# Plain attention stage: V runs one or two steps later, sixteen probability buffers, the copy of the sums two exponentials later

## What is computed

```python
qh = qh / sqrt(HD)                               # 16 heads of 16, S = 512
scores = einsum('bqhd,bhkd->bhqk', qh, kh)       # per head 512 x 512, no causal mask
attn = softmax(where(mask, scores, -inf), axis=-1)
ctx = einsum('bhqk,bkhd->bqhd', attn, vh)
x = x + (ctx @ Wo.T + bo)
```

## Time and profile before

| what | value |
|---|---|
| three runs | 2143.11, 2147.13, 2151.1 us, median 2147.13 |
| profiled execution | 2140.8 us, its span 2139.1 us |
| busy in the span | PE 81%, DVE 62%, ACT 52%, POOL 20% |
| first exponential of stage a0 | 142.97 us |
| last DVE operation of stage a0 | 493.56 us |

### The profile page before, as it was taken

The page is one execution under the profiler, slowest core; times in us unless marked ns, Lnnn a source line. Parts: engine busy times, 40 slices in busy tenths (PEclk is TensorE's granted clock), DMA queues, the critical chain, the costliest instruction groups (busy, mean ns, idle before and its releaser), DMA issues. The chain is left out here.

```text
span 2139.1 us, 40029 instructions
## 1 busy us (share of the span) xinstructions
PE 1741.3 (81%) x13902; PEld 1065.8 (50%) x13903; DVE 1331.3 (62%) x2355; ACT 1113.6 (52%) x1985; POOL 425.6 (20%) x415
## 2 busy tenths in 40 slices
PE   7659999997967999969710299999999349999987
PEld 4412222225733444437610288888888125655554
DVE  5559999984655777827844244444444367777753
ACT  6328888884525777754313233333333235565551
POOL 5200000003302233337638400000000522222000
PEclk9869999999988999987655699999999679999999
DMA  6511111102421332211268211111111421111000
GB/s 193 158 44 31 38 39 39 37 7 85 132 93 49 84 88 86 66 29 61 72 222 281 99 46 48 45 49 46 48 45 45 129 79 52 51 50 49 20 11 20
DMA packets 116771, 153.21 MB, mean 72 GB/s; under 512 B 18184, under 2 KB 96416, under 8 KB 116640
## 3 DMA queue, kind: packets, MB, share of 16 engines
q1 hardware_dynamic: 110496, 134.70, 20.2%
q0 software_dynamic: 6144, 16.79, 2.3%
HBM read 92.40 MB, written 58.53 MB: 71 GB/s over the span
## 5 line engine op out<-in xcount | busy, mean ns | idle before, releaser
L1005 ACT ACTIVATE a_prob<-a_psE 128x512 f32<-128x512 f32 (+2 forms) x896 | 453.9, 575 | 135.1 <-PE a_psE L908 132.9
L1025 DVE TENSOR_REDUCE a_nm<-a_psS 128x2 f32<-128x1024 f32 (+1 forms) x384 | 442.5, 1176 | 43.7 <-PE a_psS L886 28.7
L908 PE MATMUL a_psE<-Q,K 51*128 51x512 f16 (+3 forms) x1024 | 281.4, 347 | 32.4 <-DMA Q<-a_nrow 20.5
L886 PE MATMUL a_psS<-K,Q 49*128 49x512 f16 (+4 forms) x1024 | 267.9, 359 | 32.6 <-DVE a_nm L1025 14.8
L1643 ACT ACTIVATE ex_hf<-ex_psH,ex_b 128x256 f32<-128x256 f32 x312 | 130.7, 470 | 234.2 <-PE ex_psH L1675 234.2
L1675 PE MATMUL ex_psH<-ex_xT,ex_w1h 128*128 128x256 f16 x1872 | 231.9, 274 | 4.8 <-ACT ex_xT L1634 2.1
L924 PE MATMUL a_psO<-a_prob,vall 128*32 128x512 f32 (+3 forms) x2048 | 228.0, 529 | 3.8 <-ACT a_prob L1005 0.7
L1689 PE MATMUL ex_psY<-ex_w2h,ex_hl 128*128 x1872 | 229.5, 273 | 1.0 <-DVEq L1600 0.4
L1610 DVE CAST ex_hl<-ex_hf 128x512 f16<-128x512 f32 x156 | 66.6, 427 | 258.1 <-ACT ex_hf L1643 258.1
L908 PEld LDWEIGHTS a_psE<-Q,K 51*128 51x128 f16 x1024 | 74.9, 94 | 262.7 <-ACT a_prob L1005 166.1
L1675 PEld LDWEIGHTS ex_psH<-ex_xT,ex_w1h 128*128 x1872 | 180.5, 98 | 31.2 <-issue 9.7
(11 more groups left out here) (282 smaller groups left out, 2958.9 us busy)
## 6 DMA issues: line engine op xcount, KB each, us to landing
s_qk<-t_pk SPq DMA_DIRECT2D x32, 512.0 KB, 3.1
ex_stage<-in_w SPq DMA_DIRECT2D x16, 1024.0 KB, 5.9
s_xs<-a_zero SPq DMA_DIRECT2D x32, 312.0 KB
ex_xt<-s_xs SPq DMA_DIRECT2D x39, 256.0 KB, 2.6
s_ys<-ex_yo SPq DMA_DIRECT2D x39, 256.0 KB, 2.2
t_xin<-in_x SPq DMA_DIRECT2D x16, 512.0 KB, 4.7
K<-s_qk SPq DMA_DIRECT2D x64, 128.0 KB
Q<-s_qk SPq DMA_DIRECT2D x64, 128.0 KB
```

What stands on the lines that cost most here:

```text
L886: last = pe.matmul(psS[:, bank, col:col + n], Q6[s][at:at + SROWS, pr, t * P:(t + 1) * P], K6[s][at:at + SROWS, pr, 0:n], start=True, stop ...
L908: last = pe.matmul(psE[unit % NE][:, col:col + w], K6[s][at:at + EROWS, pr, t * P:(t + 1) * P], Q6[s][at:at + EROWS, pr, S - w:S], start=T ...
L1005: act.activation(prob[:, unit % NP_BUF, 0:w], psE[unit % NE][:, 0:w], ACT.Exp, scale=ESC).then_inc(p_ready, 1)
L1025: dve.tensor_reduce(nm[G % NM_BUF][:, t, :, i], psS[:, at:at + 2, 0:n], axis=AX.X, op=ALU.max, negate=True).then_inc(s_free, 1)
```

## The change

It has four parts, all for the plain stage: the number of `prob` buffers, the table of the V runs, the step that the code behind the loop looks up in this table (the last V run), and the exponential behind which the copy of the sums stands.

```diff
-    NP_BUF, NE, NM_BUF = 24 if causal else 12, 3, 4
+    NP_BUF, NE, NM_BUF = 24 if causal else 16, 3, 4
...
     WEIGH_AT = ({4: ((-1, 2), (-1, 3)), 10: ((0, 0),), 14: ((0, 1),)} if causal else
-                {2: ((-1, 3),), 6: ((0, 0),), 10: ((0, 1),), 14: ((0, 2),)})
+                {4: ((-1, 3),), 8: ((0, 0),), 12: ((0, 1),), 15: ((0, 2),)})
...
-            for g, t in WEIGH_AT[4 if causal else 2]:
+            for g, t in WEIGH_AT[4]:
                 weigh(G_ALL - 1, t)
...
-                    if k == (5 if causal else 3) and G > 0:
+                    if k == 5 and G > 0:
                         evacuate(G - 1)
```

## The result

The changed kernel took 2154.51 us (median of 10 runs, 2148.68 to 2157.8); the kernel before, run beside it, 2144.17 us (10 runs, 2139.03 to 2153.09). The ratio is 1.0042, 95% interval 1.0024 to 1.0061: slower, by 5 to 13 us. The forecast was 2162.8 us, 15.7 us slower.

What follows compares the result with a forecast made beforehand. No engine was full; a chain through PE, ACT and DVE set the 10.82 us group period. It would grow to 11.38: 28 x 0.56 = 15.7 us on the 2147.13 median gives 2162.8, own range 2156 to 2170, 8-in-10 range 2147 to 2172.

Steps and rivals of the forecast that it cites:

- Step (2): Turn directly behind V run 0: ends at 3.10, division starts late at 3.13, top 4 at 3.95, top 5 at 5.09.
- The ring: Chain through PE, ACT and DVE from exponential 5 to the next group's: period 11.38 instead of 10.82, 0.56 us more.
- Step (1): Copy of the sums and V run 0 move by two alike; distance from exponential to V run stays 1.12.
- Step (3): V run 2 now behind S(14), which waits for top 5: PE stands 0.52, S(15) at 7.69, top 7 at 8.14.
- Step (4): Next group's S(2) waits for top 7, then E(4), V run of step 4, exponential 5 at 11.38, closing the period.
- Steps (5) and (6): Sixteen buffers instead of twelve, and the row copy with its DMA behind the later turn: each costed at nothing.
- Step (7): First and last groups, 4 of 32, leaving 28 steady periods: ends taken as nothing, 2 us either way in the range.
- The sum: Whole forecast effect over the steady groups of stage a0: 28 x 0.56 = 15.7 us slower.
- no change: Rival: V run 2 gets past the held S(14), period 10.85, 28 x 0.03 = 1 us, time 2148; chance 0.12.
- the faster ring: Rival: DVE not late, only PE and ACT's ring counts, period 10.46, -10.1 us, time 2137.0; chance 0.06.
- The clock: Rival: PE waits more and its clock falls; half clock in a third of groups adds 26 us, 2189; chance 0.05.

Runs made afterwards that it cites:

- run 0: Not a follow-up run: V run 0 is the kernel's V run with t = 0, at step 6 in the kernel before and step 8 in the changed one.
- e5: Kernel before with only V run 1 moved, from step 10 to 12; ratio to before 0.9968 (0.9953 to 0.9984), period 10.59 us.
- e2: Kernel before with only V run 2 moved, from step 14 to 15; ratio to before 1.0049 (1.0035 to 1.0062), period 11.23 us.
- e1: Changed kernel with V run 2 back at step 14 instead of 15; ratio to before 0.9993 (0.9981 to 1.0006), period 10.78 us.
- e3: Changed kernel with twelve probability buffers instead of sixteen; ratio to before 1.0027 (1.0014 to 1.0041), period 11.06 us.
- e6: Kernel before with sixteen probability buffers instead of twelve; ratio to before 0.9998 (0.9980 to 1.0017), period 10.83 us.
- e7: Kernel before, unedited, profiled a second time; stage a0 took 375.5 us and stage a1 306.8 us.

## Why the prediction was right and wrong

The step that failed is (2): its leg from the division to top 4 (0.82 taken, 0.64 measured) and its start of the turn (1.00 behind V run 0 taken, 0.88 measured). The ring itself is the one that was forecast.

- Step (1), the distance from exponential 5 to V run 0: 316.99 - 315.86 = 1.13, forecast 1.12. Right.
- Step (2), the turn behind the V run makes the division late: the mechanism was right, two terms were mis-sized, and they are the whole miss. First, the turn was to start 1.00 behind the V run's start, the distance of a shifted score. It starts 317.87 - 316.99 = 0.88 behind it: -0.12. Second, division to top 4 was taken as 315.26 - 314.44 = 0.82 and measured 319.52 - 318.88 = 0.64: -0.18. In the kernel before that leg held a wait that I read as work: S(8) and S(9) had been held and were released together at 314.58, and top 4 came 0.45 after E(10)'s slot at 314.81, not after the recorded start of S(9). A row that the earlier trace rows leave out shows the wait, the second operation of the division in the kernel before:

```profile
314.72 0.42 DVE L1049 TENSOR_TENSOR oall<-a_psS,a_rc 128x256 f32<-128x256 f32 x1
```

It ended at 314.72 + 0.42 = 315.14, and DVE stood idle until top 4 at 315.26, 0.54 behind the start of this row. In the new order both scores are done when the division ends, and top 4 starts at once: 319.52 - 319.18 = 0.34. e5 and e2 have the held pair and legs of 0.81 and 0.79, e1 and the changed kernel have it not and show 0.64. 11.38 - 0.12 - 0.18 = 11.08; measured 11.06.
- Step (3), S(14) waits for top 5, V run 2 and S(15) behind it: right, shown by e1 and e2. PE's wait there is 0.28 (E(15) goes at 310.57, S(14) at 310.85), forecast 0.52; it shrank by most of what step (2) had too much. DVE's idle times, 0.60 and 0.35, were forecast as 0.7 and 0.4 to 0.5.
- Step (4), top 7 to S(2), E(4), the V run, exponential 5: 1.29, 0.22, 0.31, 1.42, forecast 1.28, 0.23, 0.31, 1.42. Right.
- Steps (5) and (6), buffers, row copy and its DMA: nothing, as forecast (e3, e6; E(0) is not late in the changed kernel).
- Step (7), the ends: of the last three steps between copies of the sums the first fell to 10.67 from 10.83, the next was 10.14 instead of 9.87, the last 7.79 instead of 8.62. The stage grew by 7.6 against e6 and e7, 0.9 more than the 28 periods. The forecast of nothing with 2 us either way holds.
- The sum: 28 x 0.24 = 6.7 us in place of 15.7. That the medians differ by 10.3, nearer to the forecast, is luck as far as the record shows: the steady periods give 6.7. The 0.30 us that two legs had too much in a ring of 11 us is over half of the forecast effect, since the effect is a small difference of two rings. 1.5 us for reading errors covered rounding, not a leg taken from a place where something else set its end.
- The rivals: no change and the faster ring needed S(14) not held, or half a microsecond too much on the way from the turn to S(14). S(14) was held; 0.30 was too much on that way, so the result lies between the forecast and no change. e1 shows what the new order is worth without the split pair: 10.78, little under before. The clock stayed at 1.00.

## What to carry to other kernels

When an in-order engine's program is shifted, look first at which instruction of a pair now stands behind a wait, and what long instruction comes between the two: here moving one run by one step costs or gives 0.3 to 0.4 us a group, and 15 is worse than both 14 and 16. Take a leg for a new ring only from a place where its end is set by its start; where both ends of it could be held by a third thing, look for a second place, and keep the difference in the range. Effects of 0.3% need the steady period or the stage; a profile's whole span moves by as much by itself.

## What was not expected of the hardware

- Two scores on different halves of the PE rows, held and released together, are recorded as starting within 0.01 us of each other (the rows of two at 314.58 and 313.09 in e5). The top that reads them starts 0.67 to 0.68 later, where a top that waits for its scores starts 0.45 after the second score of a pair that was not held (316.34 to 316.79). The 0.22 more is one slot. That the second score in fact goes with the shifted score that stands between them in the program fits all of these, but is inferred from DVE's starts.
- What follows a V run starts 1.00 us behind its start when it is a score, and 0.88 when it is the turn's first transposition (0.88 in e1 as well, 311.22 to 312.10). The cause was not looked into.
- The stage's first group takes 12.96 or 14.5 us in executions with the same order; the granted clock over the 15 us from the first exponential was 0.79 and 0.63 there.
